# A selective scan on one core: seven of sixteen scan inputs made by ScalarE and TensorE, and the second pair's transposes in four banks

## The reference

```
x = x + conv_block(layernorm(x))       # selective scan in 4 directions
x = x + ffn(layernorm(x))              # 8 experts, each token goes to one

# conv_block, per image, L = 1024 tokens, DI = 192 channels, N = 16 states
xh, z = split(x @ in_proj.T)           # 384 -> 2 x 192
xc = silu(depthwise_conv3x3(xh) + conv_b)
xs = 4 directions of xc: rows, columns, both also backwards
dt, B, C = split(x_proj[k] @ xs)       # 24, 16, 16 rows
delta = softplus(dt_proj[k] @ dt + bias)
for each direction k, state n:
    h[t] = h[t-1] * exp(delta[t] * A[k, n]) + (delta[t] * xs[t]) * B[n, t]
    y[t] += h[t] * C[n, t]
y = sum over directions, turned back, + D * xs
out = (layernorm(y) * g + b) * silu(z) @ out_proj.T
```

## Time and profile before

| what | value |
|---|---|
| median of 3 runs | 1870.88 us (1867.67 to 1874.52) |
| the profiled execution | 1867.9 us, span 1866.1 us |
| TensorE matmul | busy 1544.8 us, 83% of the span |
| VectorE | busy 1459.0 us, 78% |
| GpSimd | busy 1309.5 us, 70% |
| ScalarE | busy 1080.2 us, 58% |
| mean granted TensorE clock | 0.942 |

### The profile page before, as it was taken

One profiled execution on the slowest core, in us unless ns is written; L12 is line 12 of the kernel. 1 busy time (PEld: TensorE's weight loads), 2 busy tenths in 40 slices (PEclk: granted clock), 3 DMA queues, 4 the chain that ended last, 5 costly groups with the idle time before them and its releaser, 6 DMA issues.

```text
span 1866.1 us, 18341 instructions
## 1 busy us (share of the span) xinstructions
PE 1544.8 (83%) x5333; PEld 790.5 (42%) x5334; DVE 1459.0 (78%) x1564; ACT 1080.2 (58%) x1959; POOL 1309.5 (70%) x498
## 2 busy tenths in 40 slices
PE   5956887887888888995787788888788959999997
PEld 2433343333343334453343333344344645555554
DVE  5679999998999997847999999999997752233222
ACT  3877777876777754557777787777775311111110
POOL 1568999998999981416899999999997121222222
PEclk9988999998999998987799999999999969999999
DMA  3293435436434321129443543443433570111110
GB/s 122 79 323 136 132 102 180 136 99 212 133 98 147 106 80 61 52 94 326 138 135 97 177 139 98 139 142 103 132 114 102 205 263 31 47 47 43 47 51 18
DMA packets 107235, 228.00 MB, mean 122 GB/s; under 512 B 18222, under 2 KB 31057, under 8 KB 103312
## 3 DMA queue, kind: packets, MB, share of 16 engines
q1 hardware_dynamic: 102160, 213.02, 34.4%
q0 software_dynamic: 4992, 14.01, 2.4%
HBM read 183.93 MB, written 44.40 MB: 122 GB/s over the span
## 4 chain that ended last, share of the span: by engine, by line
PE 32%; DVE 24%; POOL 22%; issue 15%; ACT 3%; DMA 2%; SPq 2%; POOLq 0%; DVEq 0%; ACTq 0%
POOL arena L479 19%; DVE arena L937 15%; PE psum L1412 10%; PE psum L1431 5%; PE psum L1154 3%; DVE arena L913 3%; PE psum L1254 2%; POOL arena L464 2%; PE psum L1334 1%; DMA arena<-bc_dram 1%; SPq L346 1%; PE psum L1353 1%; PE psum L1227 1%; DVE arena L895 1%; PE psum L1280 1%
## 5 line engine op out<-in xcount | busy, mean ns | idle before, releaser
L479 POOL TENSOR_TENSOR arena<-arena 128x1536 f32<-128x1536 f32 x256 | 875.2, 3453 | 28.0 <-ACT arena L715 21.8
L1254 PE MATMUL psum<-arena,ident 128*128 128x512 f32 x1536 | 737.2, 615 | 80.7 <-POOL arena L479 80.6
L937 DVE TENSOR_TENSOR_SCAN arena<-psum,arena 128x512 f32<-128x512 f32 x528 | 614.5, 1228 | 0.0
L706 ACT ACTIVATE psum<-arena 128x512 f32<-128x512 f32 x528 | 364.2, 690 | 271.7 <-DVE arena L937 255.0
L1254 PEld LDWEIGHTS psum<-arena,ident 128*128 128x128 f32 x1536 | 280.1, 196 | 389.2 <-issue 249.9
L937 DVE TENSOR_TENSOR_SCAN arena<-arena,psum 128x512 f32<-128x512 f32 x240 | 288.3, 1237 | 17.5 <-PE psum L1280 12.1
L1280 PE MATMUL psum<-ident,arena 128*128 128x128 f32 x960 | 154.8, 289 | 144.4 <-DVE arena L937 144.4
L1280 PEld LDWEIGHTS psum<-ident,arena 128*128 128x128 f32 x960 | 118.4, 147 | 276.8 <-issue 140.2
L683 ACT ACTIVATE arena<-arena 128x192 f32<-128x192 f32 x640 | 234.6, 440 | 0.0
L464 POOL TENSOR_TENSOR arena<-arena 128x1536 f32<-128x1536 f32 x64 | 220.6, 3447 | 3.7 <-issue 3.7
L913 DVE TENSOR_TENSOR arena<-psum,arena 128x1536 f32<-128x1536 f32 x112 | 193.9, 1731 | 27.1 <-ACT psum L691 17.4
(11 more groups left out here) (163 smaller groups left out, 1516.9 us busy)
## 6 DMA issues: line engine op xcount, KB each, us to landing
arena<-bc_dram SPq DMA_DIRECT2D x864, 128.0 KB, 3.0
step_dram<-arena SPq DMA_DIRECT2D x16, 1536.0 KB, 9.3
arena<-step_dram SPq DMA_DIRECT2D x32, 768.0 KB, 7.8
arena<-in_x SPq DMA_DIRECT2D x8, 1536.0 KB, 9.2
arena<-in_w SPq DMA_DIRECT2D x6, 1876.0 KB, 11.0
t_dram<-arena SPq DMA_DIRECT2D x16, 386.0 KB, 3.8
arena<-in_w SPq DMA_DIRECT2D x4, 1536.0 KB, 12.9
z_dram<-arena SPq DMA_DIRECT2D x2, 1536.0 KB, 5.2
```

The source lines that it names most:

```text
L479: g.tensor_tensor(x, x, Cs[c % C_RING][:, None, :].to_broadcast([P, CG, HALF]), ALU.mult)\
L706: a.activation(dA[e % 2], steps[g % 2][0][:, j, :], ACT.Exp, scale=A[:, KORDER[kk], j, n:n + 1]).then_inc(s_dA, 1)
L937: v.tensor_tensor_scan(x, decay, given, 0.0 if first else state[:, n, j:j + 1], ALU.mult, ALU.add).then_inc(s_scan, 1)
L1254: ins = pe.matmul(bank[j], ident[:, :], X3[c % RING][:, j, :], start=False, stop=(n == NS - 1), skip_group_check=True)
```

## The change

The makers of the inputs are dealt out anew: P 4 to 3, D 7 to 6, A 5 to 7 of 16. ScalarE's scalings are spread over the states by a new `SCALED`, and `b_columns` takes three copies for the new columns. The transposes of x go through banks 4 to 7 instead of 0 and 1, for both pairs; for the second pair the first three sets are issued before the variance's first half and the fourth before its second, and ScalarE copies them out between its squares and roots. The wait of TensorE for `s_yc` before them is gone.

```diff
-MAKER = "PDADPDADPDADPDAA"
-BY_SCALAR = (2, 6, 10, 14, 15)
+MAKER = "PDADDAPADADAPDAA"
+BY_SCALAR = (2, 5, 7, 9, 11, 14, 15)
 LAST_D = 13
-SCALED = {15: ((2, 0, 3),), 0: ((2, 3, 8),), 2: ((6, 0, 2),), 4: ((6, 2, 8),), 6: ((10, 0, 5),),
-          8: ((10, 5, 8), (14, 0, 3)), 10: ((14, 3, 8),), 12: ((15, 0, 6),), 13: ((15, 6, 8),)}
+SCALED = {15: ((2, 0, 3),), 0: ((2, 3, 8), (5, 0, 2)), 1: ((5, 2, 5),), 3: ((5, 5, 8), (7, 0, 5)),
+          4: ((7, 5, 8),), 6: ((9, 0, 3),), 7: ((9, 3, 8),), 8: ((11, 0, 3),), 9: ((11, 3, 8),),
+          10: ((14, 0, 3),), 11: ((14, 3, 6),), 12: ((14, 6, 8), (15, 0, 6)), 13: ((15, 6, 8),)}
...
             def xT_out(p, qs):
...
-                    a.activation(xnT[b][:, k, h * HALF:(h + 1) * HALF], bank[q % 2], ACT.Copy).then_inc(s_xT, 1)
+                    a.activation(xnT[b][:, k, h * HALF:(h + 1) * HALF], bank[4 + q % 4], ACT.Copy).then_inc(s_xT, 1)
...
                 def b_columns(i):
...
-                    a.activation(BT[:, PREP[i], :, :, 0:4], cols[:, :, :, 2:15:4], ACT.Copy)
-                    a.activation(BT[:, PREP[i], :, :, 4], cols[:, :, :, 15], ACT.Copy).then_inc(s_bt, 1)
+                    a.activation(BT[:, PREP[i], :, :, 0], cols[:, :, :, 2], ACT.Copy)
+                    a.activation(BT[:, PREP[i], :, :, 1:5], cols[:, :, :, 5:12:2], ACT.Copy)
+                    a.activation(BT[:, PREP[i], :, :, 5:7], cols[:, :, :, 14:16], ACT.Copy).then_inc(s_bt, 1)
...
                     a.activation(squares[p][:, :, cs], y3[:, :, cs], ACT.Square).then_inc(s_sq, 1)
+                    if p + 1 < PAIRS:
+                        xT_out(p + 1, (2,) if h else (0, 1))
...
                     a.activation(std[:, h * HALF:(h + 1) * HALF], bank[2 + h], ACT.Sqrt, bias=eps5[:, :])\
                      .then_inc(s_std2, 1)
+                    if p + 1 < PAIRS and h == 0:
+                        xT_out(p + 1, (3,))
...
                     if p + 1 < PAIRS:
-                        xT_out(p + 1, range(4 * h, 4 * h + 4))
+                        xT_out(p + 1, range(4 * h + 4, 4 * h + 8))
...
                 if p + 1 < PAIRS:
-                    xT_out(p + 1, range(8, 12))
...
-            def rows_of_x(p):
-                for q in range(12):
+            def rows_of_x(p, qs):
+                for q in qs:
                     b, k, h = q // (2 * KC), q // 2 % KC, q % 2
                     pe.wait_ge(s_xn, p * 16 + b * TT + 4 * h + 4)
-                    if q >= 2:
-                        pe.wait_ge(s_xT, p * 12 + q - 1)
+                    if q >= 4:
+                        pe.wait_ge(s_xT, p * 12 + q - 3)
                     for t in range(4):
-                        ins = pe.transpose(bank[q % 2][:, t * P:(t + 1) * P],
+                        ins = pe.transpose(bank[4 + q % 4][:, t * P:(t + 1) * P],
...
                 for h in range(2):
+                    if p + 1 < PAIRS:
+                        rows_of_x(p + 1, (3,) if h else (0, 1, 2))
                     pe.wait_ge(s_sq, 2 * p + h + 1)
...
                 if p + 1 < PAIRS:
-                    pe.wait_ge(s_yc, 2 * p + 2)
-                    rows_of_x(p + 1)
+                    rows_of_x(p + 1, range(4, 12))
                     in_projection(p + 1)
```

More of the change, by code:

```diff
@@ L1172, in _ @@
                 if p == 0:
-                    rows_of_x(0)
+                    rows_of_x(0, range(12))
                     in_projection(0)
```

## The result

After the change the median is 1903.75 us (1898.12 to 1909.97, 4 runs), before it 1872.7 (4 runs of the same chip): ratio 1.0175, 95% interval 1.0144 to 1.0205. The profiled execution took 1902.5, with a span of 1900.5. The forecast was 1875.5 and its range ended at 1891: the change is slower by more than was allowed for.

What follows compares the result with a forecast made beforehand. VectorE and GpSimd, both full in the scan stages, were taken as the bound. Scans +13.0, between pairs -7, start -2, columns of B +0.8 make +4.8 on 1867.9; with 3.0 for the median, 1875.5 us, range 1856 to 1891.

Steps and rivals of the forecast that it cites:

- ScalarE's order: Scan stages: scalings ahead of exponentials delay VectorE's scans, 3.7 us per first half, 2.6 per second, 25.3 per pair.
- The walk through the order: State-by-state pricing in a stretch: scalings at 0.347 us each ahead of an exponential, against when VectorE wants the next scan.
- the parts outside: Outside the scan stages: -7 us between the pairs, -2 at the first pair's start, +0.8 for columns of B.
- The start: Before the first pair's scans: four banks shorten the copies of transposed x; -2 us, bounds 0 and -3.
- some slow start: Second pair's projection, starting 6.1 us earlier with less idle time before it, may be spared this; -7 us taken.
- The DMA stall at the second pair's x: First pair's scans: a 6.93 us stall at an input, x ahead of rows of B; 2 us kept, bounds 0 and 7.
- these run while VectorE scans, so I cost them at nothing.: TensorE in the scan stages: 24 more transposes for two more ScalarE-made states, priced at zero.
- the waits that stay: Scan stages: besides the DMA stall, waits of 8.7 and 11.6 us, mostly TensorE's transposes; 7 us per pair kept.
- VectorE's 16 inputs: Scan stages: VectorE makes six inputs instead of seven per stretch, 8 x 1.65 = 13.2 us less in each pair.
- The first rival: TensorE becomes late at state 5 or 7, behind a late GpSimd: 0.91 us in 16 stretches, 14.6 us, 1890; chance 0.22.
- ScalarE's delays are half absorbed: Rival: in the scan stages half of ScalarE's 50.6 us goes, 1850 (a third absorbed: 1859); chance of partly absorbed 0.18.
- the expectation of the windows: Scan-stage windows grow to 558 and 556 us; GpSimd's busy time falls to some 520, VectorE's to 524.

Runs made afterwards that it cites:

- experiment 7: Changed kernel with scalings redealt (at most six beside a VectorE input, two elsewhere), state 3's six left behind its third exponential: 1886.0 us, ratio 1.0067.
- Experiments 1: Changed kernel with state 3's eight scalings issued ahead of its third exponential, beside VectorE's input for state 4: 1869.24 us, ratio 0.9989.
- 4: Changed kernel with zero-tile products added on TensorE at the head of state 4: 1922.82 us with 24 products, 1891.5 us with 12.
- 5: Changed kernel with TensorE's additions kept two states behind through state 4, three behind only from state 5 on: 1893.51 us, ratio 1.0117.

## Why the prediction was wrong

**Right: ScalarE's order.** Forecast 50.6 us for both stages. The named waits are 38.8 (30.8 at state 4, 8.1 at states 6 to 12), but a late scan costs more than its named wait, since scans on time overlap by some 0.08 us (1.20 long, 1.118 apart). So I counted by starts: each scan's start against 1.114 us (first halves) or 1.174 (second) behind the scan before it, or 1.65 behind an input. By that the exponentials of states 3 to 12 cost 47.7 us, and 0.8 before the change: 46.9 more. The walk through the order priced each place, in first and second halves: 2.01 and 1.90 forecast at state 4, 2.05 and 1.96 measured; 0.36 and 0.15 at states 8 and 10, 0.35 and 0.14 measured; 0.45 and 0.23 at state 12, 0.42 and 0.20 measured. At state 6 half of the first halves had no such wait. Eight scalings took 2.85 us in ScalarE's timeline above, and leaving two of them out took 0.69 us off the wait (experiment 7). The Trainium skill, page "ScalarE: Activation LUTs", section "Step-by-step: what each stage is for", would by its element rate alone have made the eight an estimated 1.3 us; the rows disagree with that rate as the whole price, and they decide. The fixed part, which the prediction places in the same section, stands in the next one, "What ACT_TABLE_LOAD costs": 186 ns for an operation, 93 more for a scale or bias read from a tile, and an overlap of 93 between operations. By that page one scaling is an estimated 0.347 us and eight are 2.8, and this case's rows agree (0.347, 2.85).

**Right in sum, in part by luck: the parts outside.** The start gave 3.0 us (forecast 2), the projection starts 32.1 us after the last scan instead of 38.6, 6.4 earlier (forecast 6.1), and the convolution's copies then wait for the pad as said (timelines of TensorE and ScalarE of the changed kernel, answering):

```profile
743.61 33.81 PE L1159 MATMUL psum<-arena 128*64 128x512 f32 x144 [3.65 <-ACT arena L553]
...
751.74 1.09 ACT L559 ACTIVATE arena<-psum 128x512 f32<-128x512 f32 x2 [4.93 <-POOL arena L441]
```

Of the 6.4 only 2.4 reached the second scan stage here, 4.6 with the banks alone, where 7 was forecast. In the 11 traced kernels with the new order between the pairs, 187.1 to 191.3 us lie between the last scan of the first pair and the first of the second, against 193.7 in both with the old order; the changed kernel's trace has the 191.3. So 2.4 to 6.6 us arrive, and why it varies was not tried. It was hoped that the projection would be spared some slow start, with less idle time before it. The reverse came: it took 33.81 against 32.74, TensorE's idle time just before it rose from 0.69 to 3.65 us, and the granted clock was 0.50 in its first 4.9 us (743.6 to 748.5) and before the change in 2.5 (732.5 to 735.0). The DMA stall at the second pair's x is 3.01 and 1.04, so 4 where 2 of the 6.9 were kept. The 3.01 are a wait for GpSimd's input of state 6, which starts at 450.17, just after the row of B issued at 439.07 has landed at 450.05.

**Wrong: "these run while VectorE scans, so I cost them at nothing."** This is the step that failed. TensorE's named waits grew from 12.1 to 32.9 us. The 17.0 at states 5 and 7 were taken as none; by starts they are 21.5. The forecast treated ScalarE's delay at state 4 as VectorE's loss alone. But it also stops TensorE, in front of the one state that needs it most, and in 12 of 16 stretches TensorE comes back at half clock. A link between two terms of the sum was missing: the delay of one engine changes the price of another's work.

**Also too low: the waits that stay.** Of 20.3 us of waits without the DMA stall the forecast kept 14 and called them mostly TensorE's; only 12.1 of them are named so in the trace. At states 2, 14 and 15 the starts show 25.2 us before and 28.3 after, 3.1 more where 6.3 less was forecast: they moved from the ends to state 2 and did not shrink. The whole sum, in us for both stages, counted by starts from the first scan of each (the windows above begin at the first input and have 44.0):

```
                                   forecast   measured
VectorE's 16 inputs                  -26.4     -26.4
ScalarE's order                      +50.6     +46.9
TensorE at states 5 and 7               0      +21.5
waits at states 2, 14, 15             -6.3      +3.1
waits of inputs and at state 6        -4.9      -2.6
the rest                                0       +1.1
sum                                  +13.0     +43.6
```

**The first rival had the place and nearly the price, and not the mechanism.** It set 14.6 us at state 5 or 7, behind a GpSimd more than two products late. Experiments 1, 4 and 5 take the waits away without touching GpSimd's work. It also stood as an alternative to the forecast, while both happened. A sum of cases that exclude each other left the range too short on the slow side. "ScalarE's delays are half absorbed" is refuted: 46.9 of the 50.6 stood. One sum of the prediction is off without bearing on the result: its two windows, 558.5 and 556.1, make 69.7 us per stretch, not 69.2.

**Against the expectation of the windows:** 558 and 556 us were named, 573.5 and 572.1 came; VectorE was busy for 530 where I said 524, GpSimd for 512 where I said 520, so GpSimd had more slack than thought, and 126.0 us of its idleness lie ahead of its products (28.0 before).

## What to carry to other kernels

When work is moved onto an engine with room, price it by its place in that engine's program: beside which of the bound engine's instructions it runs, and what it stands in front of. The same 56 scalings per stretch and the same edits beside them cost 31 us or gain 18, by order alone. And where a new wait is forecast, ask of every other engine what it will do in that gap, TensorE above all, since the work behind the gap may run at half its pace.

## What was not expected of the hardware

- TensorE was granted 0.50 of its clock after 3.57 us without work in a stage whose mean was 0.96, and the transposes and additions behind took 1.08 and 1.92 us instead of 0.60 and 1.02. The length of the gap does not decide it: in the changed kernel the clock stayed at 1.00 after 3.25 us (303.92) and fell after 3.24 (591.94), and in experiment 7 it fell after 2.22 and stayed up after 2.55. What decides was not tried.
- 24 float32 products of 128x128 appeared as 48 instructions of TensorE, 5.52 us for all, 0.115 each; 12 took 2.84. TensorE's additions do the same (768 of them, 1536 instructions on the page), its transposes do not (1344 and 1344).
